# Expert stage: plain scatters of eight rows a token, ranks from routing, only the first pair turned ahead

## The chip, the cores and the metric

One core of a Trainium2 chip runs the whole program. Its engines are TensorE (PE), VectorE (DVE), ScalarE (ACT), GpSimd (POOL) and SyncE (SP, which only issues transfers here). The metric is the device time of one execution in microseconds; the median of the runs counts.

## The reference

Two layers run on 2048 tokens of width 256. The first (attention and a feed-forward) and the attention of the second are left as they are. The change is in the experts of the second layer: each token goes to 8 of 64 experts, and the weighted outputs of the 8 are added up.

```python
topk_idx, topk_w = _route(x, gate_weight, e_bias)          # 8 of 64 experts a token
w_full = zeros((T, 64)).at[arange(T)[:, None], topk_idx].add(topk_w)
def step(out, ws):                                         # scanned over the 64 experts
    wg, wu, wd, we = ws
    inter = silu(x @ wg.T) * (x @ wu.T)                    # 256 -> 176
    return (out + inter @ wd.T * we[:, None], None)        # 176 -> 256
```

## The kernel before

**Stages.** layer0 (to 559 us of the profile), layer1_front (attention output, normalisation, router logits, to 597), layer1_routing (to 661), layer1_experts (to the end). Each stage is a block: all engines meet at its end.

**Routing.** The rows of the tokens are sorted by expert into segments of 64 slots; two segments make a block of 128 rows, 160 blocks are provided (NBLK), and the routing of these inputs fills 154. DVE makes, for each of the 16 token tiles, one-hot matrices of slot column and block; ACT scales one by the token's number; PE multiplies them (L1463) into one PSUM tile of 128 x 160, whose bits give the token of each slot. DVE unpacks it (L1400 to L1411) into inv, the row that each slot gathers, and dst, the row that it is scattered to. POOL's first gathers wait for inv. The weights of experts 0 to 7 are requested in this stage.

**Experts.** A pair of blocks is one iteration m of 80. For block j POOL gathers 128 rows of x and routing weights from DRAM (L186, tile yn), PE transposes them (L1802), DVE copies the result to SBUF (L1684) and picks the weight (L1692), PE multiplies by gate and up (L1816, 16 entries in a pair), ACT takes silu (L1614), DVE multiplies (L1701), PE transposes h (L1829), multiplies down (L1841), ACT scales and copies y (L1623) into one of 8 buffers, and POOL scatters it to DRAM (L1593). ACT also copies the weights of each block's second segment (L1632, L1637), and the attention of layer 1 runs piecewise on DVE, with an exp on ACT once in 40 blocks. PE's iteration is gate/up of pair m, down of pair m-1, transposes of x of pair m+2, transposes of h of pair m; the x of pairs 0 and 1 are transposed ahead of the loop.

**POOL's order** is fixed: for i = 0, 1, ... gather block i+10 once gate/up of block i is done and the x of block i+2 has been transposed and weighed, then scatter block i-4. The scatter adds in DRAM (compute_op=ALU.add). A token has 4 rows in the scratch tensor y4, by the parity of the segment and of the block, so two scatters of one parity must not overlap, and scatter j waits until scatter j-2 has landed. y4 has to be zero at the start: SP writes the 17 pieces of zeros between layer 0's own transfers (L394).

**Weights.** SP loads expert e (L180, L182) when the blocks of expert e-16 are done; experts 8 and 9 are requested right at the start of the stage, beside the first gathers.

**The end.** PE waits for the attention, transposes and multiplies it tile by tile (L1876, L1883), DVE adds it to x_sb (L1755). When the scatters of the filled blocks have landed, SP reads y4 back in 8 pieces of 1 MB (L1574), DVE adds the 4 rows of a token for 14 of 16 tiles, two tiles an instruction (L1785, L1786, L1788); PE adds those of tiles 14 and 15 (L1904), DVE adds the sums (L1792), and ACT issues the stores of the output.

## Time and profile before

| what | us |
|---|---|
| median of 3 runs | 1225.39 (1225.15 to 1227.54) |
| the profiled execution | 1228.2 |
| its span (first to last instruction) | 1226.4 |
| PE busy | 1092.7 |
| DVE busy | 691.8 |
| ACT busy | 645.8 |
| POOL busy | 546.0 |

The profiled execution took 1.8 us more than its span and 2.8 us more than the median. Times in the rows below count from the start of the span. PE is busy for most of it, but its share differs by stage, and POOL has next to nothing to do until the experts begin.

### The profile page before, as it was taken

Reading aid. Unit: us, or ns where it says so; the run is one execution under the profiler, and the core shown is the slowest. Engines: PE = TensorE matmul, PEld = TensorE weight load, DVE = VectorE, ACT = ScalarE, POOL = GpSimd, SP = SyncE. Lnnn points to the kernel's source line nnn. Section 1 sums busy time; section 2 is a strip of 40 time slices with the busy share of each in tenths; the row PEclk is TensorE's granted clock in tenths of the full one; section 3 lists DMA queues with packets and bytes.
Section 4 is the critical chain, followed back from the end, with each engine's and each line's share of the span. In section 5 each row is a group of like instructions: output and inputs, shape, how many; then the busy total and the mean of one; then the engine's idle time right before and its main releaser. Section 6 shows DMA issues by size and latency. Waiting matters only on the chain. (4 is left out here: it accounts for less than half of the span.)

```text
span 1226.4 us, 25064 instructions
## 1 busy us (share of the span) xinstructions
PE 1092.7 (89%) x7538; PEld 655.3 (53%) x7538; DVE 691.8 (56%) x2408; ACT 645.8 (53%) x1336; POOL 546.0 (45%) x520
## 2 busy tenths in 40 slices
PE   6679999999999999998995999988988888988983
PEld 3346666666666565646663555444444444444552
DVE  6486565656566666624584656454445454454526
ACT  4215454555555545474464786665555755565640
POOL 3332222222221000003103687787877787777851
PEclk9899999999999999999897999999999998899996
DMA  7401141214121402021145659757686657875568
GB/s 237 86 27 47 30 84 31 64 31 83 31 65 32 76 25 70 19 71 40 36 130 159 168 112 226 148 99 189 110 232 131 119 111 168 187 165 105 94 121 287
DMA packets 104013, 130.16 MB, mean 106 GB/s; under 512 B 32583, under 2 KB 81991, under 8 KB 103880
## 3 DMA queue, kind: packets, MB, share of 16 engines
q1 hardware_dynamic: 68550, 77.46, 22.5%
q0 software_dynamic: 30720, 47.21, 21.6%
q10 hardware_dynamic: 4616, 3.91, 1.0%
q8 instruction: 66, 1.08, 0.4%
q14 instruction: 61, 0.50, 0.1%
HBM read 89.18 MB, written 38.97 MB: 104 GB/s over the span
## 5 line engine op out<-in xcount | busy, mean ns | idle before, releaser
L688 DVE CUSTOM_DVE_ANT_0 a_masked<-a_ps_s,a_mask 128x512 bf16<-128x512 f32 (+3 forms) x512 | 229.9, 487 | 158.7 <-PE a_ps_s L847 154.9
L1593 POOL DMA_INDIRECT y<-e_y,dst x160 | 256.5, 1603 | 76.9 <-issue 39.9
L604 ACT ACTIVATE a_probs<-a_ps_e 128x512 f32<-128x512 f32 (+1 forms) x384 | 188.3, 527 | 120.9 <-PE a_ps_e L867 119.9
L1816 PE MATMUL e_ps_gu<-e_w_gu,e_xT 128*64 x640 | 217.7, 485 | 1.1 <-DVE e_xT L1684 1.1
L1816 PE MATMUL e_ps_gu<-e_s_gu,e_xT 128*64 128x352 f32 x640 | 217.7, 485 | 0.0
L186 POOL DMA_INDIRECT yn<-rows,inv x160 | 158.6, 991 | 117.5 <-DVE inv L1405 58.9
L1841 PE MATMUL e_ps_y<-e_w_d,e_hT 88*64 x640 | 154.6, 385 | 19.7 <-issue 17.7
L1623 ACT ACTIVATE e_y<-e_ps_y,e_weight 128x256 f32<-128x256 f32 x160 | 75.0, 470 | 161.9 <-DMA y<-e_y,dst 144.0
L1841 PE MATMUL e_ps_y<-e_s_d,e_hT 88*64 88x256 f32 x640 | 154.8, 385 | 0.0
L864 PE MATMUL a_ps_e<-a_qT,a_kT 75*128 75x512 bf16 (+3 forms) x512 | 140.8, 303 | 2.1 <-ACT a_probs L604 1.8
L847 PE MATMUL a_ps_s<-a_kT,a_qT 72*128 72x512 bf16 (+3 forms) x512 | 131.2, 300 | 12.5 <-DVE a_headmax L688 11.3
L1816 PEld LDWEIGHTS e_ps_gu<-e_w_gu,e_xT 128*64 128x64 f32 x640 | 84.5, 142 | 96.4 <-issue 96.4
L1701 DVE TENSOR_TENSOR e_h<-e_sg,e_ps_gu 128x176 f32<-128x176 f32 x160 | 54.0, 338 | 142.0 <-ACT e_sg L1614 135.4
L1841 PEld LDWEIGHTS e_ps_y<-e_w_d,e_hT 88*64 88x64 f32 x640 | 85.5, 138 | 87.8 <-issue 54.0
L923 PE MATMUL a_ps_f<-a_xnT,a_w_gu 128*128 128x256 f32 x512 | 125.5, 388 | 5.6 <-DVE a_hT L713 3.3
L1632 ACT ACTIVATE e_s_gu<-e_w_gu 128x704 f32 x160 | 126.1, 789 | 6.0 <-SPq L1558 5.6
L460 POOL CAST a_m_parts<-a_negmaxT 32x128 bf16<-32x128 f32 x16 | 4.5, 281 | 276.5 <-DVE a_negmaxT L731 156.1
L1684 DVE COPY e_xT<-e_ps_xT 128x512 f32<-128x512 f32 x80 | 55.3, 691 | 104.1 <-PE e_ps_xT L1802 103.9
L867 PE MATMUL a_ps_e<-a_causal,a_identb 128*128 128x128 bf16 x512 | 112.4, 220 | 0.0
L923 PEld LDWEIGHTS a_ps_f<-a_xnT,a_w_gu 128*128 128x128 f32 x512 | 93.7, 192 | 22.8 <-DVE a_hT L713 10.8
L1802 PE MATMUL e_ps_xT<-ident_sb,yn 128*128 128x128 f32 x320 | 63.6, 302 | 42.7 <-DMA yn<-rows,inv 33.1
L1637 ACT ACTIVATE e_s_d<-e_w_d 88x512 f32 x160 | 91.0, 618 | 0.0
(234 smaller groups left out, 1808.1 us busy)
## 6 DMA issues: line engine op xcount, KB each, us to landing
e_w_gu<-e_gu SPq DMA_DIRECT2D x64, 352.0 KB
e_w_d<-e_down SPq DMA_DIRECT2D x64, 176.0 KB
a_qT<-qk_parts SPq DMA_DIRECT2D x48, 192.0 KB
y<-a_mask SPq DMA_DIRECT2D x17, 512.0 KB, 5.5
e_w_gu<-y SPq DMA_DIRECT2D x5, 1024.0 KB
qk_parts<-a_stage SPq DMA_DIRECT2D x16, 256.0 KB, 2.6
e_w_d<-y SPq DMA_DIRECT2D x3, 1024.0 KB
yn<-rows,inv POOLq DMA_INDIRECT x160, 3.0
```

The source lines that it names most:

```text
L186: eng.indirect_dma_start(self.x[:, j % self.NS, :], None, t["rows"], bass.IndirectOffsetOnAxis(inv[:, j:j + 1], 0)).then_inc(self.x_in[j % ...
L604: nc.scalar.activation(probs[:, i % HKV, UCOL[u]:UCOL[u + 1]], ps_e[:, (i * 3 + u) % 2, 0:w], ACT.Exp, scale=SCALE0).then_inc(exp_done, 1)
L688: ins = V.tensor_tensor_reduce(masked[:, n % 2, c:c + w], ps_s[:, n % 2, c:c + w], mask[:, T - w:T], 1.0, -3e38, ALU.add, ALU.max, headmax ...
L847: ins = nc.tensor.matmul(ps_s[:, x % 2, c:c + (a + 1) * P], qT[0:MROW, n % NQ, g, a * P:(a + 1) * P], kT[0:MROW, b % 2, g, 0:(a + 1) * P], ...
L864: nc.tensor.matmul(ps_e[:, x % 2, c:c + T - a * P], kT[:, b % 2, g, a * P:(a + 1) * P], qT[:, n % NQ, g, a * P:T], start=True, stop=False, ...
L867: ins = nc.tensor.matmul(ps_e[:, x % 2, c:c + P], identb[:, :], causal[:, :], start=False, stop=True, skip_group_check=True)
L923: ins = nc.tensor.matmul(ps_f[:, w * HALF:(w + 1) * HALF], w_gu[:, k, w, i * P:(i + 1) * P], xnT[:, n % NX, k, :], start=(k == 0), stop=(k ...
L1593: pool.indirect_dma_start(t["y4"], bass.IndirectOffsetOnAxis(dst[:, j:j + 1], 0), y[:, j % NY, :], None, compute_op=ALU.add).then_inc(y_ou ...
L1632: nc.scalar.activation(s_gu[:, j % 2].rearrange("p k i -> p (k i)"), w_gu[:, bass.ds(expert & (NW - 1), 1), :, :].rearrange("p a k i -> p ...
L1637: nc.scalar.activation(s_d[:, j % 2].rearrange("p k d -> p (k d)"), w_d[0:HI1, bass.ds(expert & (NW - 1), 1), :, :].rearrange("p a k d -> ...
L1816: ins = nc.tensor.matmul(ps_gu[r * SEG:(r + 1) * SEG, j % 2, 0:2 * INTER1], xT[:, j // 2 % 2, j % 2, k * P + r * SEG:k * P + (r + 1) * SEG ...
L1841: ins = nc.tensor.matmul(ps_y[r * SEG:(r + 1) * SEG, j % 2, 0:D], hT[:, j // 2 % 2, j % 2, k * P + r * SEG:k * P + (r + 1) * SEG], w.rearr ...
```

## The change

The scratch tensor y8 has a row for each token and rank (8 rows a token), and one for each slot of a block that no token fills, so no row is written twice: the scatter is a plain write, nothing is cleared in layer 0, and scatter j no longer waits for scatter j-2. The rank of a slot comes from routing: PE multiplies the one-hots of rank k into its own PSUM region (8 regions, cleared by four multiplications with a zero matrix), and DVE merges them with 7 more instructions ahead of inv; dst is 8 times the token plus the rank. The x of pair 0 alone is transposed ahead of the loop; up to m = 3 PE turns pair m+1 between gate/up and down, at m = 3 pair 5 too, and from then on pair m+2. SP waits for gathers 2 to 7 before it requests expert 8. Of 12 tiles the two rows of the lowest slots are read into qkv1 while blocks still run, once an upper bound of their slots has landed. The rest is read tile by tile, 768 KB for those 12 and 1 MB for the other 4, through 8 buffers: tile i+8 is requested when tile i is done. PE adds the rows of 6 tiles, DVE those of 10, one tile an instruction.

```diff
+EARLY_ROWS, EARLY_BATCHES = 2, 3
+EARLY_TILES = tuple(i for i in range(NT) if i % TPB < EARLY_BATCHES)
 SCATTERS = 8
...
-    "y4": ((PARTS * (TOK + P), D), F32),
+    "y8": ((TOK * TOPK + NLOAD * P, D), F32),
+    "latest": ((P,), F32),
...
@@ -388,15 +390,8 @@
-                if n == 0:
-                    sp.wait_ge(mask_in, 16)
-                if n <= NT:
-                    sp.dma_start(t["y4"].rearrange("(n p k) d -> n p k d", p=P, k=PARTS)[n],
-                                 mask[:, 0:D].rearrange("p (k d) -> p k d", k=1).to_broadcast([P, PARTS, D]))\
-                      .then_inc(y4_clear, 16)
-            sp.wait_ge(y4_clear, (NT + 1) * 16)
...
@@ -1209,7 +1207,9 @@
-        inverse = ps_inv[:, 3, 0:NLOAD]
+        def inverse(k):
+            return ps_inv[:, k // 2, k % 2 * NLOAD:(k % 2 + 1) * NLOAD]
...
@@ -1375,6 +1376,7 @@
+            ch.did(V.tensor_reduce(latest[:, :], v8[:, :, TOPK - EARLY_ROWS], AX.X, ALU.max))
...
@@ -1395,22 +1397,24 @@
                     dve.wait_ge(oh_used, (i - NOH + 1) * EIGHT)
                 equal(oh_b[i % NOH], 1, i, NLOAD, oh_ready)
+            ch.did(V.tensor_scalar(pad_row[:, :], iota[:, :], float(P), pad_id[:, 1:2], ALU.mult, ALU.add))
             dve.wait_ge(oh_used, NT * 8)
-            ch.step(V.tensor_copy(code[:, :], inverse))
+            ch.step(V.tensor_copy(code[:, :], inverse(0)))
+            for k in range(1, EIGHT):
+                ch.step(V.scalar_tensor_tensor(code[:, :], inverse(k), 4.0 ** k, code[:, :], ALU.mult, ALU.add))
             ch.did(V.tensor_scalar(is_pad[:, :], code[:, :], 0.0, None, ALU.is_equal))
             bits = code[:, :].bitcast(I32)
             ch.step(V.tensor_scalar(token[:, :], bits, 13, 2 * 1024 - 1,
                                     ALU.logical_shift_right, ALU.bitwise_and))
             V.scalar_tensor_tensor(inv[:, :], is_pad[:, :], pad_id[:, 0:1], token[:, :],
                                    ALU.mult, ALU.add).then_inc(inv_ready, 1)
-            ch.step(V.scalar_tensor_tensor(row[:, :], is_pad[:, :], pad_id[:, 0:1], token[:, :], ALU.mult, ALU.add))
-            by_parity = (x.rearrange("p (j a) -> p j a", a=2) for x in (dst[:, :], row[:, :]))
-            place, source = by_parity
-            for a in range(2):
-                ch.did(V.tensor_scalar(place[:, :, a], source[:, :, a], float(PARTS), pad_id[:, 1 + a:2 + a],
-                                       ALU.mult, ALU.add))
-            ch.last()
+            ch.did(V.tensor_scalar(rank[:, :], bits, 24, None, ALU.logical_shift_right))
+            ch.step(V.tensor_tensor(pad_row[:, :], pad_row[:, :], is_pad[:, :], ALU.mult))
+            ch.step(V.scalar_tensor_tensor(row[:, :], token[:, :], float(TOPK), rank[:, :],
+                                           ALU.mult, ALU.add))
+            ch.step(V.scalar_tensor_tensor(dst[:, :], row[:, :], -60.0, pad_row[:, :],
+                                           ALU.add, ALU.add))
...
@@ -1455,26 +1459,32 @@
+            pe.wait_ge(zeroed, 2)
+            pe.wait_ge(oh_ready, 1)
+            for b in range(4):
+                nc.tensor.matmul(ps_inv[:, b, 0:2 * NLOAD], none[:, :],
+                                 oh_b[0][:, 0:2, :].rearrange("p k c -> p (k c)"),
+                                 start=True, stop=False, skip_group_check=True)
-                nc.tensor.matmul(inverse, oh_p[:, i % 2, k, :], oh_b[i % NOH][:, k, :],
-                                 start=(j == 0), stop=(j == NT * 8 - 1), skip_group_check=True).then_inc(oh_used, 1)
+                nc.tensor.matmul(inverse(k), oh_p[:, i % 2, k, :], oh_b[i % NOH][:, k, :],
+                                 start=False, stop=(i == NT - 1), skip_group_check=True).then_inc(oh_used, 1)
...
@@ -1514,23 +1525,53 @@
-        TWO = 2 * PARTS * D
-        y4 = [spare[:, f * TWO:(f + 1) * TWO].rearrange("p (i k d) -> p i k d", i=2, k=PARTS)
-              for spare, n in ((spare_gu, 5), (spare_d, 3)) for f in range(n)]
-        rows4 = t["y4"][0:TOK * PARTS].rearrange("(i p k) d -> p i k d", p=P, k=PARTS)
+        y8 = [spare[:, f * TOPK * D:(f + 1) * TOPK * D] for spare, n in ((spare_gu, 5), (spare_d, 3)) for f in range(n)]
+        LATER = TOPK - EARLY_ROWS
+        rows8 = t["y8"][0:TOK * TOPK].rearrange("(i p k) d -> i p k d", p=P, k=TOPK)
+        early8 = qkv1[:, :, 3 * D - EARLY_ROWS * D:3 * D]
+        spare = seg_expert[0:1, 3 * P:4 * P].bitcast(F32)
+        scattered = seg_expert[0:1, 3 * P - 1:3 * P]
-        ON_PE = (NT - 2, NT - 1)
-        ON_DVE = range(NT - 2)
-        def landed(eng, f):
-            eng.wait_ge(w_in[f], NE // ring.FIRST * 32 + 16)
+        early_in, = sems(ctx, nc, "e_early_in")
+        EARLY_COUNT = 32 + len(EARLY_TILES) * 16
+        def landed_y8(i):
+            return w_in[i % NF], NE // ring.FIRST * 32 + (i // NF + 1) * 16
+        ON_PE = (1, 4, 7, 10, 12, 14)
+        ON_DVE = [i for i in range(NT) if i not in ON_PE]
         def done_of(i):
-            return (x_done_b, ON_PE.index(i) + 1) if i in ON_PE else (x_done_a, i // 2 + 1)
+            return (x_done_b, ON_PE.index(i) + 1) if i in ON_PE else (x_done_a, ON_DVE.index(i) + 1)
+        def add_up(eng, E, i, ch, done):
+            f = i % NF
+            eng.wait_ge(*landed_y8(i))
+            def fold(n, other):
+                ch.step(E.tensor_tensor(y8[f][:, 0:n * D], y8[f][:, 0:n * D], other, ALU.add))
+            if i in EARLY_TILES:
+                fold(EARLY_ROWS, early8[:, i, :])
+                fold(LATER - 4, y8[f][:, 4 * D:LATER * D])
+            else:
+                fold(4, y8[f][:, 4 * D:8 * D])
+            fold(2, y8[f][:, 2 * D:4 * D])
+            fold(1, y8[f][:, D:2 * D])
+            eng.wait_ge(o_added, ON_DVE.index(i) + 1)
+            E.tensor_tensor(x_sb[:, i, :], x_sb[:, i, :], y8[f][:, 0:D], ALU.add).then_inc(done, 1)
+        CATCH_UP = 3
+        def turned_behind(m):
+            return [q for q in ((m + 1,) if m < CATCH_UP else (m + 1, m + 2) if m == CATCH_UP else (m + 2,))
+                    if q < PAIRED]
...
@@ -1553,25 +1594,46 @@
-            def weights_in(e):
+            def landed(e):
                 sp.wait_ge(w_in[e % ring.FIRST], (e // ring.FIRST + 1) * 32)
                 sp.sem_inc(w_ready, 1)
             for e in range(ring.FIRST - 1):
-                weights_in(e)
+                landed(e)
+            for j in range(ring.SOON, NS):
+                sp.wait_ge(x_in[j], 16)
             for e in range(ring.FIRST, NE):
                 if e >= NW:
                     blocks = sp.value_load(last[0:1, e - NW:e - NW + 1], min_val=1, max_val=NBLK)
                     sp.wait_ge(y_ready, blocks)
                 ring.load(sp, t, e)
-                weights_in(e - 1)
-            weights_in(NE - 1)
+                landed(e - 1)
+                if e == ring.FIRST + 1:
+                    sp.dma_start(t["latest"].rearrange("(p a) -> p a", a=1), latest[:, :],
+                                 allow_slow_non_contiguous=True).then_inc(early_in, 16)
+                if e == NW - 1:
+                    sp.wait_ge(early_in, 16)
+                    sp.dma_start(spare, t["latest"].rearrange("(a p) -> a p", a=1)).then_inc(early_in, 16)
+            landed(NE - 1)
+            sp.wait_ge(y1_ready, EARLY_BATCHES * B)
+            first_rows = sp.value_load(scattered, min_val=16, max_val=NBLK // NY * 16)
+            for b in range(NY):
+                sp.wait_ge(y_out[b], first_rows)
+            for i in EARLY_TILES:
+                sp.dma_start(early8[:, i, :].rearrange("p (k d) -> p k d", d=D), rows8[i, :, LATER:TOPK, :])\
+                  .then_inc(early_in, 16)
             counts = [sp.value_load(filled[0:1, b:b + 1], min_val=16, max_val=NBLK // NY * 16) for b in range(NY)]
             for b in range(NY):
                 sp.wait_ge(y_out[b], counts[b])
-            for f in range(ring.FIRST):
-                sp.dma_start(y4[f], rows4[:, 2 * f:2 * f + 2]).then_inc(w_in[f], 16)
+            for i in range(NT):
+                f = i % NF
+                if i >= NF:
+                    sp.wait_ge(*done_of(i - NF))
+                n = LATER if i in EARLY_TILES else TOPK
+                sp.dma_start(y8[f][:, 0:n * D].rearrange("p (k d) -> p k d", d=D), rows8[i, :, 0:n, :])\
+                  .then_inc(w_in[f], 16)
...
@@ -1587,11 +1649,8 @@
-                if j >= 2:
-                    pool.wait_ge(y_out[(j - 2) % NY], ((j - 2) // NY + 1) * 16)
-                pool.indirect_dma_start(t["y4"], bass.IndirectOffsetOnAxis(dst[:, j:j + 1], 0),
-                                        y[:, j % NY, :], None, compute_op=ALU.add).then_inc(y_out[j % NY], 16)
+                pool.indirect_dma_start(t["y8"], bass.IndirectOffsetOnAxis(dst[:, j:j + 1], 0),
+                                        y[:, j % NY, :], None).then_inc(y_out[j % NY], 16)
...
@@ -1754,23 +1813,29 @@
-            for m in range(2):
-                copy_x(m)
-                for j in (2 * m, 2 * m + 1):
-                    weigh(j)
+            copy_x(0)
+            weigh(0)
+            weigh(1)
-                if m + 2 < PAIRED:
-                    copy_x(m + 2)
+                for q in turned_behind(m):
+                    copy_x(q)
-                if m + 2 < PAIRED:
-                    weigh(j + 4)
-                    weigh(j + 5)
-                if j == COUNTED_AT:
+                for q in turned_behind(m):
...
@@ -1778,18 +1843,15 @@
-            for f in range(NT // 2):
-                if 2 * f in ON_PE:
-                    continue
-                landed(dve, f)
-                ch.step(V.tensor_tensor(y4[f][:, :, 0:2, :], y4[f][:, :, 0:2, :], y4[f][:, :, 2:4, :], ALU.add))
-                ch.step(V.tensor_tensor(y4[f][:, :, 0, :], y4[f][:, :, 0, :], y4[f][:, :, 1, :], ALU.add))
-                dve.wait_ge(o_added, 2 * f + 2)
-                V.tensor_tensor(x_sb[:, 2 * f:2 * f + 2, :], x_sb[:, 2 * f:2 * f + 2, :], y4[f][:, :, 0, :], ALU.add)\
-                 .then_inc(x_done_a, 1)
-            for n, i in enumerate(ON_PE):
-                dve.wait_ge(summed, n + 1)
-                V.tensor_tensor(x_sb[:, i, :], x_sb[:, i, :], ps_gu[:, n % 2, 0:D], ALU.add).then_inc(x_done_b, 1)
+            dve.wait_ge(early_in, EARLY_COUNT)
+            for i in range(NT):
+                if i in ON_DVE:
+                    add_up(dve, V, i, ch, x_done_a)
+                else:
+                    n = ON_PE.index(i)
+                    dve.wait_ge(summed, n + 1)
+                    V.tensor_tensor(x_sb[:, i, :], x_sb[:, i, :], ps_gu[:, n % 2, 0:D], ALU.add)\
+                     .then_inc(x_done_b, 1)
...
@@ -1845,8 +1907,11 @@
-            for j in range(4):
-                transpose_x(j)
+            def turn_pair(m):
+                for j in (2 * m, 2 * m + 1):
+                    transpose_x(j)
+            turn_pair(0)
+                if m <= CATCH_UP:
+                    turn_pair(m + 1)
-                if m + 2 < PAIRED:
-                    for j in two:
-                        transpose_x(j + 4)
+                if m >= CATCH_UP and m + 2 < PAIRED:
+                    turn_pair(m + 2)
-            order = list(ON_DVE) + list(ON_PE)
+            order = ON_DVE + list(ON_PE)
...
@@ -1892,17 +1958,22 @@
+            pe.wait_ge(early_in, EARLY_COUNT)
+                f = i % NF
-                landed(pe, i // 2)
-                for k in range(PARTS):
-                    ins = nc.tensor.matmul(ps_gu[:, n % 2, 0:D], ident[:, :], y4[i // 2][:, i % 2, k, :],
-                                           start=False, stop=(k == PARTS - 1))
+                pe.wait_ge(*landed_y8(i))
+                for k in range(TOPK):
+                    row = y8[f][:, k * D:(k + 1) * D]
+                    if i in EARLY_TILES and k >= LATER:
+                        row = early8[:, i, (k - LATER) * D:(k - LATER + 1) * D]
+                    ins = nc.tensor.matmul(ps_gu[:, n % 2, 0:D], ident[:, :], row,
+                                           start=False, stop=(k == TOPK - 1))
```

On POOL, in the loop of the expert stage, a gather (yn) and a scatter (from e_y by dst) take turns. Before, the scatters to y4, from the third on, wait for a landing (e_y_out) too:

```order
L1593 DMA y4<-e_y,dst 8704x256 [waits e_y_copied]
L186 DMA yn<-rows,inv 128x320 [waits e_weighed,e_gu_ready,e_xT_ready]
L1593 DMA y4<-e_y,dst 8704x256 [waits e_y_out0,e_y_copied]
L186 DMA yn<-rows,inv 128x320 [waits e_weighed,e_gu_ready,e_xT_ready]
L1593 DMA y4<-e_y,dst 8704x256 [waits e_y_out1,e_y_copied]
L186 DMA yn<-rows,inv 128x320 [waits e_weighed,e_gu_ready,e_xT_ready]
L1593 DMA y4<-e_y,dst 8704x256 [waits e_y_out2,e_y_copied]
```

And of the changed kernel:

```order
L188 DMA yn<-rows,inv 128x320 [waits e_weighed,e_gu_ready,e_xT_ready] x5
L1652 DMA y8<-e_y,dst 36864x256 [waits e_y_copied]
L188 DMA yn<-rows,inv 128x320 [waits e_weighed,e_gu_ready,e_xT_ready]
L1652 DMA y8<-e_y,dst 36864x256 [waits e_y_copied]
L188 DMA yn<-rows,inv 128x320 [waits e_weighed,e_gu_ready,e_xT_ready]
```

The order of gathers and scatters is the same; the waits for e_y_out are gone from this engine. On PE, at the start of the expert stage, the transposes of x (e_ps_xT) and the first gate/up of block 0 (e_ps_gu) stood like this:

```order
L1802 MATMUL e_ps_xT<-ident_sb,yn 128x128 [waits e_x_in0]
L1802 MATMUL e_ps_xT<-ident_sb,yn 128x128
L1802 MATMUL e_ps_xT<-ident_sb,yn 128x128 [waits e_x_in1]
L1802 MATMUL e_ps_xT<-ident_sb,yn 128x128
L1802 MATMUL e_ps_xT<-ident_sb,yn 128x128 [waits e_xT_copied,e_x_in2]
L1802 MATMUL e_ps_xT<-ident_sb,yn 128x128
L1802 MATMUL e_ps_xT<-ident_sb,yn 128x128 [waits e_x_in3]
L1802 MATMUL e_ps_xT<-ident_sb,yn 128x128
L1807 TENSOR_LOAD seg_expert
L1807 ISA x2
L1807 TENSOR_LOAD seg_expert
```

And now:

```order
L1864 MATMUL e_ps_xT<-ident_sb,yn 128x128 [waits e_x_in0]
L1864 MATMUL e_ps_xT<-ident_sb,yn 128x128
L1864 MATMUL e_ps_xT<-ident_sb,yn 128x128 [waits e_x_in1]
L1864 MATMUL e_ps_xT<-ident_sb,yn 128x128
L1869 TENSOR_LOAD seg_expert
L1869 ISA x2
L1869 TENSOR_LOAD seg_expert
L1869 ISA x2
L1878 REGISTER_ALU [waits e_w_copied,e_xT_copied]
```

The transposes that wait for gathers 2 and 3 (e_x_in2, e_x_in3) have moved behind the first pair's gate/up.

## Rows read from the trace of the kernel before

**Rows 1.** Page, part 1: busy us (share of the span) and instructions of each engine.

```profile
PE 1092.7 (89%) x7538; PEld 655.3 (53%) x7538; DVE 691.8 (56%) x2408; ACT 645.8 (53%) x1336; POOL 546.0 (45%) x520
```

**Rows 2.** Chain that ended last: start us, us, what; gate/up of pairs 1, 2 and 7.

```profile
677.26 2.52 PE e_ps_gu L1816 x16
...
682.53 2.52 PE e_ps_gu L1816 x16
...
710.14 2.52 PE e_ps_gu L1816 x16
```

**Rows 3.** Timeline of POOL: start us, us, line, operation [idle before it].

```profile
692.35 1.57 POOL L1593 DMA_INDIRECT y<-e_y,dst  x1 [0.30 <-issue]
694.23 0.99 POOL L186 DMA_INDIRECT yn<-rows,inv  x1 [0.30 <-issue]
```

**Rows 4.** Groups by line on POOL, expert stage: busy us, mean ns, idle before.

```profile
L1593 POOL DMA_INDIRECT y<-e_y,dst x160 | 256.5, 1603 | 76.9 <-issue 39.9 <-ACT e_y L1623 23.0 <-DMA y<-e_y,dst 12.7
L186 POOL DMA_INDIRECT yn<-rows,inv x158 | 156.4, 990 | 58.3 <-issue 37.2 <-DVE e_pick L1692 7.9 <-PE e_ps_gu L1816 5.7
```

**Rows 5.** Waits in the expert stage: us in total, times, longest us.

```profile
ACT e_y L1623 <- DMA y<-e_y,dst: 144.0, 73, 5.7
...
PEld e_ps_xT L1802 <- DMA yn<-rows,inv: 45.2, 45, 4.2
```

**Rows 6.** Timeline at the start of the expert stage, POOL and PE.

```profile
656.41 1.21 POOL L186 DMA_INDIRECT yn<-rows,inv  x1 [58.93 <-DVE inv L1405]
...
661.14 1.08 PE L1802 MATMUL e_ps_xT<-ident_sb,yn 128*128 128x128 f32 x4 [6.20 <-PEq L1157]
...
671.02 0.84 PE L1816 MATMUL e_ps_gu<-e_w_gu,e_xT 128*64 x1 [1.15 <-DVE e_xT L1684]
...
677.19 0.51 PE L1816 MATMUL e_ps_gu<-e_w_gu,e_xT 128*64 x1
```

**Rows 7.** Timeline of the routing: PE's sums in PSUM, DVE's last steps.

```profile
621.54 2.65 PE L1448 MATMUL d_ps_inv<-d_selb,l_sums 128*128 128x512 bf16 x15
...
655.09 0.38 DVE L1405 SCALAR_TENSOR_TENSOR inv<-d_is_pad,l_ids,d_token 128x160 uint32<-128x160 f32 x1
```

**Rows 8.** Timeline of the end, engine by engine: PE, ACT, DVE, SP.

```profile
1171.38 0.51 PE L1816 MATMUL e_ps_gu<-e_w_gu,e_xT 128*64 x1
...
1179.21 0.38 PE L1841 MATMUL e_ps_y<-e_w_d,e_hT 88*64 x1
...
1216.39 3.78 PE L1904 MATMUL e_ps_gu<-e_w_d,ident_sb 128*128 128x256 f32 x8 [17.25 <-DMA e_w_d<-y]
...
1182.03 0.47 ACT L1623 ACTIVATE e_y<-e_ps_y,e_weight 128x256 f32<-128x256 f32 x1 [2.77 <-DMA y<-e_y,dst]
...
1184.00 0.42 DVE L1755 TENSOR_TENSOR x_sb<-x_sb,e_ps_o 128x256 f32<-128x256 f32 x1 [7.01 <-PE e_ps_o L1883]
1185.08 0.42 DVE L1755 TENSOR_TENSOR x_sb<-x_sb,e_ps_xT 128x256 f32<-128x256 f32 x1 [0.66 <-PE e_ps_xT L1883]
...
1198.43 1.22 DVE L1785 TENSOR_TENSOR e_w_gu<-e_w_gu 128x1024 f32<-128x1024 f32 x1
1199.68 0.69 DVE L1786 TENSOR_TENSOR e_w_gu<-e_w_gu 128x512 f32<-128x512 f32 x1
...
1223.77 0.42 DVE L1792 TENSOR_TENSOR x_sb<-x_sb,e_ps_gu 128x256 f32<-128x256 f32 x1 [3.14 <-PE e_ps_gu L1904]
...
1186.45 2.94 SPq L1574 DMA_DIRECT2D e_w_gu<-y  x5
```

**Rows 9.** Stretches: PE, PEld, DVE, ACT, POOL busy (x), PEclk, DMA share, GB/s.

```profile
700.00:713.00 13.00, 11.96 (x92) 6.70 (x90) 7.52 (x24) 11.52 (x23) 10.56 (x9) 1.00 0.55 93
735.00:765.00 30.00, 27.41 (x208) 15.45 (x204) 17.97 (x50) 19.89 (x41) 21.80 (x18) 1.00 0.88 217
1166.00:1186.00 20.00, 15.87 (x112) 9.38 (x111) 5.22 (x14) 9.91 (x23) 13.45 (x9) 1.00 0.49 60
1190.00:1200.00 10.00, 9.14 (x51) 7.52 (x49) 4.82 (x10) 3.09 (x9) 3.41 (x3) 1.00 1.03 356
```

38 lines of the change are left out of this document (26 added, 12 removed).

## Prediction

> **What bounds the kernel now.** I read the page first: PE is busy 89% of the span, POOL 45% [rows 1], but POOL's share all lies in the last 570 us. So the question is who sets the pace of the expert stage, which begins with the first gate/up at 671.02 us [rows 6] and ends for PE at 1179.4 [rows 8]: 508.4 us for 80 pairs, 6.35 us a pair. PE alone would need 5.27: that is the distance of two pairs' gate/up in the chain [rows 2], with no gap on PE between them. POOL's timeline shows the other 1.08 us. A gather holds it 0.99 us, a scatter 1.58, and before each it takes 0.30 to start although it waits for nothing [rows 3]: 0.99 + 0.30 + 1.58 + 0.30 = 3.17 us a block, 6.35 a pair. That is the pace of the stage to the hundredth, so POOL bounds it. The waits agree: PE waits for gathers and ACT for the landing of scatters, 144 us in 73 waits [rows 5], both behind the queue on POOL. Transfers are not the bound: their share is 0.55 where no weights are loaded and 0.88 in the heaviest stretch [rows 9]. After the loop comes a tail of 47 us: attention added on DVE (one tile in 1.08 us), 8.4 MB read back from 1186.45 to 1216.4, the rows added, tiles 14 and 15 last on PE at half clock [rows 8].
>
> **Layer 0.** 17 transfers of zeros go, and their issues on SP. PE is busy there and no wait for them ends anything, so I count 0; a gain of up to 1 us is possible from SP's freer queue.
>
> **Routing, later by 3.5 us.** Seven scalar_tensor_tensor of 128 x 160 stand before inv. The one in the trace takes 0.38 us [rows 7]; with 0.03 between dependent ones 7 x 0.41 = 2.9. Four clearing matmuls of 320 columns: 15 of 512 columns took 2.65 us [rows 7], 0.177 each, so at most 4 x 0.177 = 0.7 and by columns 0.45; I take 0.6, all of it on PE's path. The steps behind inv and the reduction for the bound run beside POOL's first gathers. The first gather moves from 656.41 to 659.9.
>
> **Start of the experts, earlier by 4.9, then 3.8.** Now PE turns four blocks before the first gate/up, and the last of them lands only at 669.2. With one pair ahead only gather 1 counts: issued at 661.4, landed in some 2.9 us as most of them (the first ones beside weights took up to 6, and these are now requested later), 664.3; transposes at half clock 0.9, copy 0.7, so the first gate/up is at 666.1 instead of 671.02. What is late next: pair 1's copy now follows DVE's two products of pair 0, so PE waits about 1.1 us there. Second gate/up at 673.4 instead of 677.19 [rows 6].
>
> **The scatters, the large term.** What a plain scatter costs POOL no row shows. The nearest row on one side is the plain gather, 0.99 us, on the other the adding scatter, 1.58 (mean 1.60) [rows 3, 4]. Both move 128 rows of about 1 KB by an index; the adding one has to read two operands for each row that it writes, and it costs more by 0.6. The plain scatter has one read and one write a row, as the gather has, so I take 0.99 and keep 0.95 to 1.58 as bounds. POOL's period is then 4 terms: 0.99 + 0.30 + 0.99 + 0.30 = 2.58 us a block, 5.16 a pair, just below PE's 5.27: PE becomes the bound, with 2% of margin. The GPSIMD Engine Reference of the Trainium skill (When to use GPSIMD) says that a pair of cores makes the descriptors, one those that read and one those that write; by that rule a plain scatter and a plain gather cost the same, 0.99, and the stage would come out as in my sum. No run here shows it yet.
>
> From the second gate/up 78 more pairs are 78 x 5.272 = 411.2 us. Once in 40 blocks ACT changes tables for the exp: the six pairs from 677.26 to 710.14 took 32.88, which is 1.25 above 6 x 5.272 [rows 2]; four times, 5.0. For gathers that come late in bursts of weights I add 3. The last gate/up is then at 673.4 + 411.2 + 5.0 + 3 = 1092.6 instead of 1171.38 [rows 8]: 78.8 earlier. The loop's end keeps its 8.0 us and comes at 1100.6. POOL must not fall back: gathers run 10 blocks ahead, so some 9 us of delay are absorbed.
>
> **The tail, longer.** Attention: the first add came 4.6 us after the loop's end, 2.8 of them ACT's wait for a landing [rows 8]; without it 1102.5. Ten adds instead of 14: 9 x 1.083 + 0.42 = 10.2, end 1112.7. Reading back: block 153, the last filled, is down-multiplied at about 1088, scattered and landed at 1092, so SP starts about there and not at 1186. The first 8 tiles are 6.8 MB; at the 356 GB/s of the saturated stretch [rows 9], with pad scatters beside them, 22 us, 1114: they are there as DVE wants them. The early 3.1 MB are read around block 133, where only transfers have to make room. So DVE sets the pace: 1024 columns 1.25 us from start to start, 512 columns 0.72, 256 some 0.42 [rows 8]. An early tile is 3 x 0.72 + 0.45 + 0.42 = 3.03, another 1.25 + 0.72 + 0.45 + 0.37 = 2.79; 7 and 3 of them, and 6 x 0.45 for PE's tiles: 32.3. PE's first tile is ready 1.4 after DVE wants it; its tile 14 (16 matmul entries, which are 7.6 us at the 0.47 each of the half clock [rows 8], half of it at full clock) may cost 0 to 3: 1.5. The last add ends at 1112.7 + 32.3 + 1.4 + 1.5 = 1147.9, and the last store adds the 2.2 us that it took before (1224.2 to 1226.4). Span 1150.1. Tail after the loop: 49.5 instead of 47.0, although the reading starts before the loop's end.
>
> **Sum.** 1226.4 - 78.8 (loop, start included) + 2.5 (tail) = 1150.1 us of span. The profiled execution stood 1.8 above its span and 2.8 above the median, so the median is the span less 1.0: **1149 us**.
>
> **Rivals.**
> (a) *The plain scatter is dearer on POOL than a gather, but cheaper than the adding one.* Above 1.05 us POOL is the bound again; each 0.1 us is 0.1 x 146 = 14.6 us: 1.25 us would give 1149 + 29 = 1178. At 1.58, with the waits for scatter j-2 gone, the loop would have 146 x 3.17 = 464 us from the first scatter (681) instead of 477.8: last gather at 1144, end about 1210. For it: no row shows a plain scatter. Against: the second operand.
> (b) *The transfers become the bound.* Without weights a gather and a scatter need 0.55 x 3.17 = 1.74 us of the 16 engines; a scatter alone, from nine in 20 us at 0.49, 1.09; a gather so 0.65 [rows 9]. Weights: the stretch from 735 to 765 has ten experts in it and 0.88, (26.4 - 16.4) / 10 = 1.0 an expert at most, 0.40 a block. With unchanged scatters 2.14 of PE's 2.64, 81%; in a burst of ten experts more than the time there is. Each of some three bursts could then hold PE up by 5: 1149 + 15 = 1164. Against: a plain scatter should need less than 1.09.
> (c) *DVE or PE in the tail is slower than counted* (half clock on all six of PE's tiles, 6 x 3.8 above, half of it hidden): 1149 + 11 = 1160.
> (d) *Slower than before.* The plain write costs POOL more than the adding one, because the write side and not the second read is what takes 1.58. At 1.58 with all the old waits kept, only the start (-3.8 and the tail's +2.5 and up to 3 more for clock) differ: 1227. Each 0.1 above adds 14.6, so at 1.7 it is 1244. It decides from 1.58 us on. Against it: gathers write 128 rows too, in 0.99.
> (e) *The first pair's move brings nothing*, since gather 1 lands late beside other transfers: 1149 + 4 = 1153, inside the forecast.
>
> **Chances and range.** Forecast with (e) 0.70, 1138 to 1160; (a) 0.13, 1160 to 1212; (b) 0.08, 1155 to 1172; (c) 0.05, 1155 to 1162; (d) 0.04. The range has to reach into (a) and (b): 1137 to 1172. About 0.2% (2.5 us) is what a measurement of this kernel can tell from no change. Faster by more than that 0.94, within it 0.02, slower 0.04.
>
> **What the next profile would show.** Right: the plain scatter at 0.95 to 1.05 us on POOL, at most a few us of "DMA y" waits on ACT, gate/up of consecutive pairs 5.27 apart nearly everywhere with the granted clock at 1.0, first gate/up near 666, last near 1093, DVE busy without gaps from 1113 to 1148. Wrong: a scatter at 1.2 or more and a POOL without gaps while PE waits for yn (a); transfer share above 0.9 and gathers that land in over 7 us, PE waiting for them (b); DVE waiting for e_summed or for a landing in the tail (c).

## The result, and the profile after

The changed kernel takes 1145.2 us (median of 4 runs, 1142.0 to 1147.0) against 1226.5 for the kernel before: a ratio of 0.933, 95% interval 0.929 to 0.936. The forecast was 1149, its range 1137 to 1172. The profiled execution took 1147.0 with a span of 1145.2, where the working had 1150.1.

The first part of its page answers [rows 1]. PE does nearly the same work (84 instructions more), but it was busy 89% of the span and is now busy 94%; POOL's busy time falls by 92 us:

```profile
PE 1075.8 (94%) x7622; PEld 662.4 (58%) x7622; DVE 704.3 (61%) x2448; ACT 655.3 (57%) x1336; POOL 454.3 (40%) x521
...
PEclk9899999999999999999999989999999999999999
```

The groups by line on POOL answer [rows 4], and the summary of the scatter's own line gives the spread (duration in ns: least, median, most):

```profile
L188 POOL DMA_INDIRECT yn<-rows,inv x160 | 159.0, 994 | 118.9 <-DVE inv L1410 60.0
L1652 POOL DMA_INDIRECT y<-e_y,dst x160 | 163.9, 1024 | 59.1 <-issue 28.3
```

```profile
L1652 POOL DMA_INDIRECT y<-e_y,dst x160: 966/992/2014, 688.1 to 1099.6; - x160
```

The plain scatter costs POOL 0.99 us in the median and 1.02 in the mean, where the adding one cost 1.58 and 1.60. The gather costs 0.97 and 0.99. POOL's timeline in the middle of the stage, against [rows 3], shows the new period: 0.97 + 0.30 + 0.99 + 0.30, a block from 766.41 to 768.99, 2.58 us.

```profile
766.41 0.99 POOL L1652 DMA_INDIRECT y<-e_y,dst  x1 [0.30 <-issue]
767.71 0.97 POOL L188 DMA_INDIRECT yn<-rows,inv  x1 [0.30 <-DVE e_pick L1751]
768.99 0.99 POOL L1652 DMA_INDIRECT y<-e_y,dst  x1 [0.30 <-PE e_ps_gu L1878]
```

And the chain of the work that ended last, against [rows 2] (start, duration, what):

```profile
667.43 4.33 PE e_ps_gu L1878 x16
...
673.88 2.59 PE e_ps_gu L1878 x16
...
679.50 2.52 PE e_ps_gu L1878 x16
...
685.05 2.52 PE e_ps_gu L1878 x16
...
691.16 2.52 PE e_ps_gu L1878 x16
...
713.47 2.52 PE e_ps_gu L1878 x16
...
718.74 2.52 PE e_ps_gu L1878 x16
...
1085.99 2.52 PE e_ps_gu L1878 x16
1090.81 2.52 PE e_ps_gu L1878 x16
```

After the first pairs, gate/up follows gate/up every 5.27 us (713.47, 718.74), which is PE's own time for a pair. Only four pairs differ, those at which ACT changes tables for the exp, 6.50 each, and the last distance, 4.82, in which no x is left to turn. ACT's 144 us of waits for landings [rows 5] are gone altogether. A stretch of 50 us (columns as in [rows 9]) shows it in one line: PE 50.00 of 50, the clock at 1.00, the transfers at 0.60.

```profile
950.00:1000.00 50.00, 50.00 (x384) 28.98 (x381) 29.87 (x88) 37.52 (x78) 38.63 (x38) 1.00 0.60 180
```

From the second gate/up to the last it was 494.2 us and is now 416.9, 77.3 less. That is nearly the whole gain of 81.

How much POOL has to spare is seen in its groups by line from 700 us to the last gather (busy us, mean ns, idle before):

```profile
L1652 POOL DMA_INDIRECT y<-e_y,dst x141 | 144.3, 1024 | 43.0 <-issue 24.4 <-ACT e_y L1682 8.5 <-PE e_ps_gu L1878 7.6
L188 POOL DMA_INDIRECT yn<-rows,inv x142 | 141.6, 997 | 43.3 <-issue 30.5 <-PE e_ps_gu L1878 7.0 <-DVE e_pick L1751 5.8
```

Busy and idle time add up to the whole stretch, and no gap is longer than 0.31 us. By the medians POOL needs 5.15 us a pair; by the means, in which eleven operations of 1.3 to 1.64 us count, 5.26. PE needs 5.27, and 5.34 with the changes of tables (416.9 / 78). So POOL works through its queue without a pause too and has little to spare. PE still waits for no gather there; they run ten blocks ahead.

### The profile page after: what moved, and what is told of

Its sections match the earlier page's. It is cut to its first block and busy times, and to the rows that moved or that the text cites. A ratio compares the mean times of both kernels' runs of the same rounds, so it can differ in the third digit from the quotient of the medians.

```text
span 1145.2 us, 25135 instructions
## 1 busy us (share of the span) xinstructions
PE 1075.8 (94%) x7622; PEld 662.4 (58%) x7622; DVE 704.3 (61%) x2448; ACT 655.3 (57%) x1336; POOL 454.3 (40%) x521
## 3 DMA queue, kind: packets, MB, share of 16 engines
q0 software_dynamic: 15360, 47.21, 13.0%
## 5 line engine op out<-in xcount | busy, mean ns | idle before, releaser
L1878 PE MATMUL e_ps_gu<-e_w_gu,e_xT 128*64 x640 | 208.2, 468 | 2.5 <-ACT e_s_gu L1691 1.6
L1878 PE MATMUL e_ps_gu<-e_s_gu,e_xT 128*64 128x352 f32 x640 | 208.2, 468 | 0.0
L1652 POOL DMA_INDIRECT y<-e_y,dst x160 | 163.9, 1024 | 59.1 <-issue 28.3
L1903 PE MATMUL e_ps_y<-e_w_d,e_hT 88*64 x640 | 151.5, 379 | 0.9 <-DVE e_hT L1768 0.9
L1903 PE MATMUL e_ps_y<-e_s_d,e_hT 88*64 88x256 f32 x640 | 151.5, 379 | 0.0
L1878 PEld LDWEIGHTS e_ps_gu<-e_w_gu,e_xT 128*64 128x64 f32 x640 | 81.6, 137 | 91.9 <-issue 91.0
L1673 ACT ACTIVATE e_sg<-e_ps_gu 128x176 f32<-128x176 f32 x160 | 50.7, 317 | 77.3 <-PE e_ps_gu L1878 72.5
L859 PEld LDWEIGHTS a_ps_e<-a_qT,a_kT 75*128 75x128 bf16 x512 | 49.2, 97 | 75.1 <-ACT a_probs L599 67.3
```

The lines of the kernel that those rows point to most:

```text
L859: nc.tensor.matmul(ps_e[:, x % 2, c:c + T - a * P], kT[:, b % 2, g, a * P:(a + 1) * P], qT[:, n % NQ, g, a * P:T], start=True, stop=False, ...
L1652: pool.indirect_dma_start(t["y8"], bass.IndirectOffsetOnAxis(dst[:, j:j + 1], 0), y[:, j % NY, :], None).then_inc(y_out[j % NY], 16)
L1878: ins = nc.tensor.matmul(ps_gu[r * SEG:(r + 1) * SEG, j % 2, 0:2 * INTER1], xT[:, j // 2 % 2, j % 2, k * P + r * SEG:k * P + (r + 1) * SEG ...
L1903: ins = nc.tensor.matmul(ps_y[r * SEG:(r + 1) * SEG, j % 2, 0:D], hT[:, j // 2 % 2, j % 2, k * P + r * SEG:k * P + (r + 1) * SEG], w.rearr ...
```

## The experiments

Times are medians, and code is shown in part. The kernel before ran beside each kernel on the same chip, and a ratio is to that. Three kernels ran twice, on two chips, for a reason that the results make plain.

### One word, in the kernel before

before_plain: the adding scatter made plain, nothing else. Rows that should be added up are then overwritten, so its sums are wrong; the work is the same.

```
-                                        y[:, j % NY, :], None, compute_op=ALU.add).then_inc(y_out[j % NY], 16)
+                                        y[:, j % NY, :], None).then_inc(y_out[j % NY], 16)
```

> The kernel before with one word less: its scatters are plain, all else stays (y4 and its clearing, four rows a token, the wait for scatter j-2, two pairs turned ahead, routing, tail). Rows that should be added are overwritten, so the sums of a token's experts are wrong; the work is the same otherwise. Theory P (POOL's 1.58 us for an adding scatter was the bound, a plain one takes 0.99): the scatters on POOL show about 0.99, gate/up of consecutive pairs stand 5.27 apart from 677.19 on, 78 x 5.272 + 5 = 416 us instead of 494, ACT's waits for a landing are gone; the start and the tail (47 us) are those of before: 1226.5 - 78 = 1148 us. Theory W (what held the loop was the wait for the landing of scatter j-2, which stays here): the loop stays above 6 us a pair and the time above 1200. Theory S (much of the gain came from the new start and from reading back early): over 1160.

### The price put back, in whole and in half

adding_all makes every scatter of the changed kernel add, adding_half those of odd blocks only; both clear y8 in layer 0. Of adding_all:

```
+                for c in ((n, NT + 1) if n == 0 else (n,)):
+                    sp.dma_start(t["y8"].rearrange("(n p k) d -> n p k d", p=P, k=16)[c],
...
-                                        y[:, j % NY, :], None).then_inc(y_out[j % NY], 16)
+                                        y[:, j % NY, :], None, compute_op=ALU.add).then_inc(y_out[j % NY], 16)
```

> The changed kernel, but every scatter adds (into y8, which 18 more transfers in layer 0 fill with zeros, 37.7 MB; each row is still written once, so nothing is left out of the computation). No wait for scatter j-2, new start, new tail. Theory P: POOL is the bound again at 0.99 + 0.30 + 1.58 + 0.30 = 3.17 us a block, 6.35 a pair; the last gate/up comes 494 us after the second instead of 417, at about 1168; the reading back begins behind the last scatter of a full block, about 15 us later, and the 22 us of its first eight tiles are no longer hidden beside the loop: 1222 us (1212 to 1230). Theory W: 1145 to 1155, since the wait is gone. If the clearing slows layer 0, the whole is later by that; the loop is read by itself.

> The changed kernel with adding scatters for odd blocks and plain ones for even blocks (y8 cleared in layer 0 as in adding_all; nothing is left out). Theory P: POOL needs 2.58 + 3.17 = 5.75 us a pair against PE's 5.27, 0.48 too much; over 76 pairs that is 36 us, of which the gathers' lead of ten blocks swallows some 10 at the start: the last gate/up some 26 us later than 1090.8 and, with the reading back later too, 1145 + 30 = 1175 us (1165 to 1185). A loss in proportion to the number of adding scatters (half of that of adding_all, 38) would speak for a cost on each scatter's own transfer rather than for two engines of which the slower one sets the pace. Theory W: 1145 to 1150.

### The wait for the landing of scatter j-2 put back

wait_kept:

```
+                if j >= 2:
+                    pool.wait_ge(y_out[(j - 2) % NY], ((j - 2) // NY + 1) * 16)
```

> The changed kernel, plain scatters, with one thing put back: before scatter j POOL waits for the landing of scatter j-2. Nothing is left out. Theory P: a scatter lands within some 3 us and scatter j-2 was issued two blocks, 5.2 us, before, so the wait is over when it begins: same as the change, 1145 us within 2. Theory W: the gain came from dropping this wait, and much of it goes again: over 1180.

**What these four gave, on one chip.** adding_all 1224.8 us, ratio 0.999 (0.996 to 1.002), as expected by theory P. But before_plain 1264.0 (ratio 1.031), adding_half 1259.4 (1.028) and wait_kept 1269.7 (1.038): three kernels slower than the kernel before. Theory W's bounds (over 1200, over 1180) hold for before_plain and wait_kept, but W has adding_all at 1145 to 1155 and adding_half at 1145 to 1150, so no theory fits all four. The kernel before stood at 1227.8 beside them. POOL's plain scatters had the price expected (1.00 us in wait_kept), and POOL was busy only 36% of that span. The timeline of wait_kept shows what was wrong:

```profile
702.75 0.66 PE L1867 MATMUL e_ps_xT<-ident_sb,yn 128*128 128x128 f32 x4
...
703.24 0.60 PE L1894 MATMUL e_ps_hT<-ident_sb,e_h 128*88 128x128 f32 x4
...
709.99 0.47 ACT L1685 ACTIVATE e_y<-e_ps_y,e_weight 128x256 f32<-128x256 f32 x1 [5.22 <-remote]
...
712.83 0.69 DVE L1746 COPY e_xT<-e_ps_xT 128x512 f32<-128x512 f32 x1 [9.98 <-remote]
714.31 0.69 DVE L1771 COPY e_hT<-e_ps_hT 88x512 f32<-88x512 f32 x1 [0.78 <-remote]
```

PE's transposes of x end at 703.4 by PE's row, and the copy that waits for nothing else starts at 712.83; "remote" says that the profile has no releaser for it. The copy of hT, for which PE's rows end at 703.84, comes at 714.31. In all, DVE waited so 98 us before e_xT and 9 before e_hT, and ACT 109 us. PE then ran dry, and the granted clock of a stretch fell to 0.90:

```profile
900.00:950.00 50.00, 43.53 (x296) 24.07 (x293) 23.77 (x70) 28.25 (x60) 30.46 (x30) 0.90 0.50 156
```

In adding_all POOL's rows settle what paces it: from 690 us to the end POOL has no gap above 0.32 us, and two blocks take 6.35 in the median, as expected. Two of them:

```profile
900.04 0.99 POOL L188 DMA_INDIRECT yn<-rows,inv  x1 [0.30 <-issue]
901.35 1.58 POOL L1659 DMA_INDIRECT y<-e_y,dst  x1 [0.31 <-issue]
903.23 0.99 POOL L188 DMA_INDIRECT yn<-rows,inv  x1 [0.30 <-issue]
904.52 1.58 POOL L1659 DMA_INDIRECT y<-e_y,dst  x1 [0.30 <-issue]
```

I had no theory for the unexplained waits, so the next question was whether they belonged to these kernels or to the occasion.

### The changed kernel again, a harmless wait, the old start

wait_four waits for scatter j-4 instead of j-2. start_old turns two pairs ahead, on PE and DVE, and drops SP's wait for x_in 2 to 7:

```
-            for j in range(ring.SOON, NS):
-                sp.wait_ge(x_in[j], 16)
...
             turn_pair(0)
+            turn_pair(1)
```

> The changed kernel itself, once more, because three kernels with plain scatters (before_plain, wait_kept, adding_half) came out at 1259 to 1270 us where 1148, 1145 and 1175 were expected, and in each of them DVE and ACT wait up to 10 us for signals of PE that PE's rows show as given long before. Theory C (that is the chip or the moment, and hits every kernel with plain scatters there): 1255 to 1275 us, with the same unexplained waits. Theory K (it is in those three kernels: the waits for landings that they keep, or the adding scatters that they have): 1145 us within 3, no such waits.

> The changed kernel with a wait before scatter j for the landing of scatter j-4, four blocks and over 10 us before, so that it is over when it begins. Nothing is left out. Theory K with the landing as its cause (a plain scatter lands later than 5.2 us after its issue, so that waiting for j-2 holds POOL): 1145 us within 3. Theory K with the wait instruction itself as its cause: like wait_kept, about 1270. Theory C: as after_again, whatever that is.

> The changed kernel with the start of the kernel before: two pairs of x turned ahead of the first gate/up, and SP's requests for weights 8 and up not held behind the first gathers. Nothing is left out. By the prediction's step the start is worth 3.8 us at the second gate/up, and the catching up behind it gives about 1.5 of it back: 1145 + 2 to 5 = 1147 to 1150 us if the rest of the loop runs as in the profile of the change. If the order at the start decides whether the loop keeps PE's pace at all (rival), this run is above 1200 while after_again is at 1145. Theory C: as after_again.

**Measured, on a second chip.** after_again 1149.7 us (ratio 0.934, 0.929 to 0.938), wait_four 1149.5 (0.935), start_old 1153.9 (0.939, 0.935 to 0.943). In none of them does an unexplained wait stand. So the change holds on another chip, and the wait for scatter j-4 costs nothing that shows. The old start costs 4.2 us by the medians; the intervals of the two ratios overlap, so its price rests on the timelines. Blocks are counted from 0: gather 3 was issued at 666.59 and PE waits for it until 672.54:

```profile
664.74 1.09 PE L1863 MATMUL e_ps_xT<-ident_sb,yn 128*128 128x128 f32 x4 [8.78 <-PEq L1152]
...
670.12 0.69 PE L1863 MATMUL e_ps_xT<-ident_sb,yn 128*128 128x128 f32 x2 [4.29 <-DMA yn<-rows,inv]
672.54 0.69 PE L1863 MATMUL e_ps_xT<-ident_sb,yn 128*128 128x128 f32 x2 [1.73 <-DMA yn<-rows,inv]
674.41 0.84 PE L1877 MATMUL e_ps_gu<-e_w_gu,e_xT 128*64 x1 [1.18 <-DVE e_xT L1741]
```

The first gather itself falls anywhere from 657.3 to 664.6 us in kernels whose work ahead of it is the same, so starts are compared from there. From the first gather to the second gate/up it is 20.7 us in start_old and 14.6 in after_again; from there to the last, 415.7 against 417.1. The new start is worth 6.0 us and gives 1.4 back: 4.6.

### The three once more, and the tail

The same three kernels under new names, and two_on_pe:

```
-        ON_PE = (1, 4, 7, 10, 12, 14)
+        ON_PE = (7, 14)
```

> wait_kept once more, on another occasion. On the first one the unexplained waits of DVE and ACT began at 674 us, 15 us before the first scatter, where wait_kept and the changed kernel do the same; so the wait for scatter j-2 can't have started them. Theory C (that chip or that moment held PE's signals back in every kernel that works PE without pauses; after_again and wait_four were run elsewhere): where the chip is another one, 1147 us within 4, ratio to the kernel before 0.935. Theory W (the wait for the landing of scatter j-2 does it): about 1270 again, ratio 1.035.

> adding_half once more, on another occasion. Theory C: it was held by the same thing; on an undisturbed chip POOL needs 5.75 us a pair against PE's 5.27, 36 us in all, some 10 of them swallowed by the lead of the gathers: 1145 + 30 = 1175 us (1165 to 1185), ratio 0.955. A cost in proportion to the number of adding scatters would give the middle between 1147 and 1225, 1186. Theory W, or anything in the kernel itself: about 1259 again.

> before_plain once more, on another occasion (rows that should be added are overwritten, so a token's sums are wrong; the work is the same). Theory C with P: gate/up 5.27 apart from 677 on, 1226.5 - 78 = 1148 us, ratio 0.936. Theory W: about 1264 again, ratio 1.03.

> The changed kernel with two tiles (7 and 14) summed by PE at the end instead of six; nothing is left out. Its expert loop is that of the change, so it also tells whether this chip runs such a loop undisturbed. By the step on the tail DVE sets the pace there: four more attention adds, 4 x 1.083 = 4.3, and four more tiles of some 3.0 - 0.45 = 2.55 on DVE, 10.2: 1147 + 14.5 = 1161.5 us (1158 to 1165), DVE without gaps. If instead the reading back sets the pace (rival), the time stays within 3 of the changed kernel's 1145 to 1150.

**Measured, on a third chip.** before_plain_b 1148.9 us (ratio 0.935, 0.930 to 0.939), adding_half_b 1181.4 (0.959, 0.953 to 0.964), wait_kept_b 1162.8 (0.947, 0.942 to 0.951), two_on_pe 1161.2 (0.945, 0.941 to 0.949). No unexplained waits in any.

What follows, one by one:

*before_plain_b.* One word in the kernel before brings 78.9 us, where 78 was expected; its chain shows PE's pace from pair 1 on:

```profile
681.59 2.52 PE e_ps_gu L1816 x16
...
686.86 2.52 PE e_ps_gu L1816 x16
...
692.13 2.52 PE e_ps_gu L1816 x16
```

Together with adding_all this closes the case for the price. The price alone gives the gain of the whole change (0.935 against 0.933), and all the rest of the change without the price gives nothing (0.999). That 78.9 stands so near 78 is in part luck, since the expectation left start and tail as they were. By the traced executions the loop from the second gate/up to the last became 75.0 us shorter (419.2, where 416 was expected), the second gate/up came 4.3 later, 2.8 of it with the first gather, and from PE's end of the loop to the end it took 38.3 us instead of 46.8: the reading back starts 2.5 us behind PE's end instead of 6.8 and takes 25.8 us instead of 29.9. The changed kernel reads and adds twice as many rows, and its tail takes 46.7, 8.4 more than this one; its new start and the dropped wait make up for that.

*adding_half_b.* From the second gate/up to the last it took 448.4 us: 31.6 more than the change, while adding_all took 490.3, 73.4 more. Two engines of which the slower sets the pace gave 36 less what the gathers' lead swallows; I had put that at 10, and it was about 5. Proportion gave 36.7. The time (1181.4) lies between the two forecasts, 1175 and 1186, so it doesn't tell them apart. The rows do: a gather follows the last but one after 5.78 us in the median, from 698 us on POOL has no gap above 0.35 us, and PE still keeps 5.27 from pair 7 to pair 16, while the gathers' lead lasts. A cost on each scatter's own transfer would not wait for that. At this pace ACT waits for landings again, which it never did in the change:

```profile
ACT e_y L1692 <- DMA y<-e_y,dst: 94.5, 61, 4.1
```

*wait_kept_b.* 1162.8 instead of 1147: the wait for scatter j-2 isn't free at the new pace. I was wrong there. The waits of POOL and ACT, and then one stretch with a burst of weights (columns as in [rows 9]), of wait_kept_b:

```profile
POOL y L1655 <- DMA y<-e_y,dst: 29.2, 51, 6.2
...
ACT e_y L1685 <- DMA y<-e_y,dst: 36.0, 23, 3.4
```

```profile
865.00:885.00 20.00, 18.35 (x135) 10.07 (x136) 9.16 (x31) 10.35 (x23) 12.82 (x14) 1.00 0.90 283
```

The same stretch of the changed kernel:

```profile
865.00:885.00 20.00, 20.00 (x154) 11.58 (x152) 11.66 (x33) 14.82 (x32) 15.43 (x16) 1.00 0.85 260
```

With the transfers at 0.90, scatter j-2 has not always landed when scatter j is due. POOL stands, and since by its means it has next to nothing to spare it doesn't catch up: it issued 14 operations there instead of 16. The eight buffers of y run out, ACT waits, and PE idles 1.65 us in these 20. From the second gate/up to the last it took 427.9 us instead of 416.9. In before_plain_b, with the same wait but the old order at the start, the loop took 419.2 against start_old's 415.7, 3.5 more. So the wait cost 3.5 to 11 us in the loop; why the two differ I can't say. Each is one execution, and that of wait_kept_b is the fastest of its four, which spread from 1156.4 to 1166.7.

*two_on_pe.* 1161.2, expected 1161.5. From PE's end of the loop to the last add it takes 58.2 us instead of 44.6 of the change: 13.7 more, expected 14.5. DVE sets the pace of the tail.

### Reading back without the early part

late_rows: `EARLY_TILES = (0,)` instead of 12 tiles.

> The changed kernel with the early reading taken away for 11 of its 12 tiles: only tile 0 has two of its eight rows read beside the loop, all other rows are read at the end. Nothing is left out. The prediction counted the early reading as free (3.1 MB less to read at the end for 0.2 us more on DVE for each early tile). Without it the first eight tiles are 8.1 MB instead of 6.9, at 356 GB/s 23 us from 1088.7, so still there when DVE wants tile 0 at 1110.5 to 1112; the other eight are 1.05 MB each, 2.95 us a tile, slower than DVE and PE use them up (32.4 / 16 = 2.0): tile 15 comes at about 1114 + 8 x 2.95 + 2 = 1140 instead of in time, DVE saves 11 x 0.15 = 1.6: 1145 to 1149 by the forecast's steps plus 0 to 3, so 1146 to 1152 and ratio 0.935 to 0.939, with DVE waiting a few us for landings behind tile 8. Rival (the early reading is what keeps the tail short, by much): over 1156.

**Measured, on a fourth chip.** 1146.4 us, ratio 0.933 (0.929 to 0.937): the same as the change. DVE waits for no landing behind tile 8. The step that failed in this expectation is the 356 GB/s. The stretches of late_rows show more, once no gathers or scatters run beside:

```profile
1100.00:1110.00 10.00, 10.00 (x56) 8.63 (x55) 4.81 (x11) 3.08 (x9) 0.00 (x0) 1.00 0.99 416
...
1120.00:1125.00 5.00, 4.47 (x22) 3.61 (x21) 4.79 (x10) 0.38 (x1) 0.00 (x0) 1.00 1.01 421
```

At 420 GB/s a tile of 1.05 MB takes an estimated 2.5 us and not 2.95. Reading early brings nothing here that can be measured.

### What stays open

What kept DVE and ACT waiting on the first chip isn't known. Settled is this: the code alone doesn't do it, since the same three kernels gave 1270, 1264 and 1259 us there and 1163, 1149 and 1181 on the third chip. Whether it was the chip or the moment was not tried. It hit the three kernels with plain scatters, all or half of them. adding_all, on the same chip, has just two such waits, 2.2 and 2.1 us, that end at 675.71 and 686.14, and came out at 1225; the kernel before stood at 1228 there, as elsewhere. So it goes with kernels in which PE works at its own pace, but that is argued from five kernels and not shown. It began before the first scatter (DVE's first such wait in wait_kept ends at 674.38, the first scatter starts at 689.54), so no wait of a scatter can have started it. Where it lasted longest, POOL was working without a pause, from 696.46 to 712.59. But the changed kernel has POOL without a pause nearly throughout, and no such wait.

The Trainium skill (SBUF — State Buffer, section Who interferes with whom) says that GpSimd and a DVE copy in a two-port mode lock each other out for a whole instruction, and that a DVE instruction outside these modes with at most one input from SBUF doesn't contend with GpSimd. Nothing shows these copies, which read PSUM, in such a mode: 512 columns take 0.69 us, as long as a tensor_tensor of 512 columns (0.69), which by the same section has no two-port mode. In the change 114 of DVE's 160 such copies start inside one of POOL's operations without an unexplained wait, and they take no longer than the others (0.68 against 0.69 us). And ACT, which by the page has ports of its own, waited as long (109 us against DVE's 107). So that lock doesn't explain it. Whether the changed kernel itself would have been hit on that chip was not tried.

## Why the prediction was right

**POOL's price carries it.** The sum rested on 0.99 us for a plain scatter, taken from the gather. It is 0.99 in the median (1.02 in the mean), and the runs show both directions of it: before_plain_b 0.935 with it alone, adding_all 0.999 without it. The GPSIMD Engine Reference of the Trainium skill (When to use GPSIMD) says that of a pair of cores one makes the descriptors that read and the other those that write. By that rule a plain scatter costs what a gather costs, and the trace agrees within 0.03 us: 992 ns against 972 in the median, 1024 against 994 in the mean. Rival (a) and rival (d) fall with the same row, and adding_half_b bears out the threshold of (a): above PE's 5.27 us a pair POOL is the bound again.

**The margin was mis-sized.** The sum took 0.99 us for a scatter and had POOL 2% below PE. The median is that, but some operations take 1.3 to 1.64, and by the means POOL's pair is 5.26 against 5.27, 0.2%. It did no harm here: behind the first pair PE waits for no gather.

**Term by term**, all on the profiled execution (forecast, measured):

| step | forecast | measured |
|---|---|---|
| first gather | 659.9 | 659.66 |
| first gate/up | 666.1 | 667.43 |
| second gate/up | 673.4 | 673.88 |
| last gate/up | 1092.6 | 1090.81 |
| PE's end of the loop | 1100.6 | 1098.4 |
| first attention add | 1102.5 | 1100.45 |
| attention adds end | 1112.7 | 1110.6 |
| last add ends | 1147.9 | 1143.0 |
| span | 1150.1 | 1145.2 |

*Routing.* The seven steps from PSUM took 2.47 us together, where I had 2.9, and the four clearing matmuls 0.7 (0.6):

```profile
655.42 2.47 DVE L1405 SCALAR_TENSOR_TENSOR d_code<-d_ps_inv,d_code 128x160 f32<-128x160 f32 x7
...
658.36 0.38 DVE L1410 SCALAR_TENSOR_TENSOR inv<-d_is_pad,l_ids,d_token 128x160 uint32<-128x160 f32 x1
```

inv comes 3.3 us later than in [rows 7]. One run can't confirm that by the clock time: the first gather wanders by 7 us between runs.

*Start.* The direction held and start_old gives its price, 4.2 us of median. Two parts were off. I had DVE and the gather as what is late; it was ACT, whose copy e_s_gu starts at 666.29, 1.5 us behind PE's first transposes, so the first gate/up is 1.3 later. PE reaches full clock during pair 0 (an entry takes 0.79 us up to 670.4 and 0.46 from 670.97; before, it took 0.79 through the whole pair), which takes back 0.8 of it. And the three pairs behind the first, up to the one in which two pairs of x are turned, take 5.62, 5.55 and 6.11 us instead of 5.27: 1.5 us that my sum didn't have (starts 673.88, 679.50, 685.05, 691.16 above).

```profile
666.29 1.47 ACT L1691 ACTIVATE e_s_gu<-e_w_gu 128x704 f32 x2 [8.21 <-issue]
```

*Loop.* 78 x 5.272 and the four changes of tables (I had 5.0; 4 x 1.23 = 4.9) hold. The 3 us that I set aside for late gathers weren't needed: behind the first pair PE waits for no gather. The last distance is 4.82, 0.45 less than counted. Against these stand the second gate/up, 0.5 late, and the 1.5 of catching up. That is nearly all of the 1.8 us by which the last gate/up comes sooner.

*Tail.* DVE is the bound, as forecast. Its rows: an early tile is 0.72 + 1.91 + 0.34 from start to start, 2.97 us against my 3.03; it waits once, 1.14 us, for PE's first tile (I had 1.4).

```profile
1110.54 0.69 DVE L1557 TENSOR_TENSOR e_w_gu<-e_w_gu,qkv 128x512 f32<-128x512 f32 x1
1111.26 1.88 DVE L1557 TENSOR_TENSOR e_w_gu<-e_w_gu 128x512 f32<-128x512 f32 x3
1113.17 0.42 DVE L1567 TENSOR_TENSOR x_sb<-x_sb,e_w_gu 128x256 f32<-128x256 f32 x1
1114.74 0.42 DVE L1853 TENSOR_TENSOR x_sb<-x_sb,e_ps_gu 128x256 f32<-128x256 f32 x1 [1.14 <-PE e_ps_gu L1975]
```

The 1.5 us for PE at half clock were not needed: its last tile runs at full clock (12 entries in 2.75 us, where 8 took 3.78 in [rows 8]), and the longest idle time of PE ahead of it is 0.95 us, where it was 17.25. Rival (c) falls with it. The terms were too high by 1.0 on DVE's sum, 0.3 on the wait and 1.5 on the clock, together 2.8.

*Reading back.* SP starts at 1088.7 (forecast 1092), and the first eight tiles are there when DVE wants them. (6.8 MB at 356 GB/s would be 19 us; the working had 22.) I counted the early rows as free; late_rows shows that they are also of no use.

**What the prediction did not have.** Its sum gave the removed wait for scatter j-2 no value of its own. wait_kept_b shows that this was luck of the wording: with the price gone but the wait kept, 13 to 18 us come back. The row for it was there: in [rows 4] POOL waits 12.7 us for landings of scatters even at the old pace of 6.35 us for two blocks, and at the new pace two blocks take 5.27. The whole change is right on either reading, because it removes both. Where the prediction did price the wait, in rival (a), it was half right: for 1.58 us a scatter without the waits it has a loop of 464 us from the first scatter instead of 477.8, and an end near 1210. adding_all is that kernel. From its first scatter to its last gather it takes 465.2 us, but the first scatter starts at 689.3 and not at 681, and it came out at 1224.8.

Rival (b), the transfers as the bound, is seen in part: not by themselves, since in one of the heaviest stretches of the change their share is 0.92 and PE is busy for all 20 us. With that wait PE does lose time at such shares.

```profile
875.00:895.00 20.00, 20.00 (x154) 11.57 (x152) 10.77 (x34) 14.90 (x31) 15.13 (x17) 1.00 0.92 289
```
